# Silu behind its own half of the projections, final sums and store in halves, and one chunk's statistics moved behind the scan loop

## What is computed

```python
x = x + 0.5 * moe(layernorm(x))       # silu(x @ Wg.T) * (x @ Wu.T) @ Wd.T, weighted per expert
x = x + scan_block(layernorm(x))
x = x + 0.5 * moe(layernorm(x))
x = x + 0.5 * ffn(layernorm(x))       # (silu(x @ Wg.T) * (x @ Wu.T)) @ Wd.T
x = x + attention(layernorm(x))
x = x + 0.5 * ffn(layernorm(x))
```

## Time and profile before

| | us |
|---|---|
| median of the 3 runs | 1901.24 |
| lowest and highest | 1899.95, 1901.25 |
| the profiled execution, its own time | 1902.52 |
| its span, first to last instruction | 1900.7 |
| PE busy | 1808.4 (95%) |
| DVE busy | 1333.8 (70%) |
| ACT busy | 945.2 (50%) |
| POOL busy | 581.2 (31%) |

### The profile page before, as it was taken

How to read it: one execution, slowest core, us unless ns; L and a number is a source line. 1 busy time by engine, 2 the same in 40 slices (tenths; PEclk the granted TensorE clock), 3 DMA queues, 4 the chain that set the end, 5 groups by cost and what they waited for, 6 DMA issues and landing times.

```text
span 1900.7 us, 26241 instructions
## 1 busy us (share of the span) xinstructions
PE 1808.4 (95%) x9417; PEld 1375.2 (72%) x9417; DVE 1333.8 (70%) x1870; ACT 945.2 (50%) x1782; POOL 581.2 (31%) x399
## 2 busy tenths in 40 slices
PE   7999999999799999988689999999999999999998
PEld 6888888888354544534267888888888887777887
DVE  6666656567999999999976666565675556666533
ACT  3442323333688677684445433233333338888422
POOL 1000234000489878888720000000000025555000
PEclk9999999999899999999999999999999999999999
DMA  5332344220222222223202233232121306553100
GB/s 197 90 98 66 97 145 136 64 62 23 67 73 70 69 72 77 71 71 108 72 17 76 72 95 105 65 104 63 64 77 44 65 1 147 109 109 68 37 12 23
DMA packets 84186, 146.39 MB, mean 77 GB/s; under 512 B 13848, under 2 KB 23704, under 8 KB 83544
## 3 DMA queue, kind: packets, MB, share of 16 engines
q1 hardware_dynamic: 84056, 144.72, 26.6%
HBM read 130.38 MB, written 14.29 MB: 76 GB/s over the span
## 4 chain that ended last, share of the span: by engine, by line
PE 72%; DVE 14%; issue 6%; ACT 4%; POOL 3%; DMA 0%; DVEq 0%; SPq 0%; POOLq 0%; ACTq 0%
PE psum L161 19%; PE psum L162 18%; PE psum L163 18%; DVE scan_state L1618 6%; PE psum L1437 5%; POOL scan_state L1208 2%; PE psum L1990 1%; PE psum L1361 1%; DVE scan_state L1625 1%; PE psum L1332 1%; ACT attn_p L2138 1%; DVE X L807 1%; DVE moe_hidden_lo L850 1%; PE psum L1421 1%; PE psum L278 1%
## 5 line engine op out<-in xcount | busy, mean ns | idle before, releaser
L1208 POOL TENSOR_TENSOR scan_state<-scan_delta_u,scan_B_rows 128x1024 f32<-128x1024 f32 x127 | 299.5, 2368 | 95.3 <-PE psum L1437 81.2
L161 PE MATMUL psum<-xnT_hi,moe_w_hi 128*128 128x512 f32 x800 | 316.5, 396 | 2.7 <-DVE xnT_lo L470 2.6
L778 ACT ACTIVATE moe_hidden<-psum 128x512 f32<-128x512 f32 x200 | 119.5, 597 | 393.9 <-PE psum L163 393.9
L162 PE MATMUL psum<-xnT_lo,moe_w_hi 128*128 128x512 f32 x800 | 314.2, 393 | 0.0
L163 PE MATMUL psum<-xnT_hi,moe_w_lo 128*128 128x512 f32 x800 | 312.0, 390 | 0.0
L1618 DVE TENSOR_TENSOR_SCAN scan_state<-psum,scan_state 128x1024 f32<-128x1024 f32 x128 | 292.2, 2283 | 4.2 <-POOL scan_state L1208 3.0
L827 DVE TENSOR_TENSOR moe_gated_up<-moe_gate_rows,psum 128x512 f32<-128x512 f32 x184 | 126.5, 688 | 210.0 <-PE psum L163 124.8
L1437 PE MATMUL psum<-scan_state,ident 128*128 128x512 f32 x512 | 248.1, 608 | 3.8 <-DVE scan_gated L1633 2.6
L418 POOL TENSOR_SCALAR rstd<-mean_var 128x2 f32<-128x2 f32 x48 | 10.5, 220 | 752.8 <-DVE mean_var L452 752.5
L161 PE MATMUL psum<-moe_w_hi,moe_hidden_hi 128*128 128x256 f32 x800 | 230.4, 288 | 3.9 <-DVE moe_hidden_lo L850 2.6
L163 PE MATMUL psum<-moe_w_hi,moe_hidden_lo 128*128 128x256 f32 x800 | 226.3, 283 | 0.0
(11 more groups left out here) (226 smaller groups left out, 3476.4 us busy)
## 6 DMA issues: line engine op xcount, KB each, us to landing
scan_B_rows<-scan_B SPq DMA_DIRECT2D x127, 256.0 KB, 3.1
moe_gate_rows<-gate_table SPq DMA_DIRECT2D x176, 128.0 KB, 3.0
moe_w_raw<-moe_pack SPq DMA_DIRECT2D x50, 384.0 KB, 4.0
attn_stack<-attn_rows SPq DMA_DIRECT2D x96, 128.0 KB, 5.3
moe_gate_rows<-gate_table SPq DMA_DIRECT2D x32, 224.0 KB, 3.1
ffn_w_raw<-ffn_pack SPq DMA_DIRECT2D x16, 384.0 KB, 3.6
moe_gate_rows<-gate_table SPq DMA_DIRECT2D x32, 160.0 KB, 2.6
moe_gate_rows<-gate_table SPq DMA_DIRECT2D x24, 192.0 KB, 2.8
```

Of the source, the lines that this page charges most:

```text
L161: e.matmul(out, wH, xH, start=start, stop=False)
L162: e.matmul(out, wH, xL, start=False, stop=False)
L778: e.activation(self.hb[:, b, :], self.k.psum[:, 2 * b, :], ACT.Silu).then_inc(self.s_silu.sem, 1)
L1208: e.tensor_tensor(self.st[q % self.NBUF][:], self.dtu[:, 2 * h:2 * h + 2, :], self.Bs[:, q % self.RING, :].unsqueeze(1).broadcast_to([P, 2 ...
```

## The change

It has three parts. (1) In every Glu step the gate half of the projection raises a semaphore of its own, `s_gs`, and Silu waits for that; the multiplication of line 835 now waits for `s_gu` too. (2) In the last stage the last `down` raises `s_half` after its sixth matmul, and the last `take` adds half 0 behind that and half 1 behind `s_dn`; the last chunk is stored by two transfers of 256 KB, each behind its own add. (3) The statistics of chunk 1 of the tail between scan and second MoE leave the scan loop: DVE does them after the last `gate`, before the last adds; POOL's part goes to the start of the MoE stage's list, and ACT's normalisation (line 293, four instructions) behind the Silu of the MoE stage's step 0.

```diff
--- before.py
+++ after.py
@@ -404,11 +404,16 @@
 
     def sync(self, e):
 
-        for c in range(NCH):
+        for c in range(NCH - 1):
             e.wait_ge(self.s_add.sem, self.s_add.at(2, c))
             e.dma_start(self.out[c * CHUNK:(c + 1) * CHUNK, :].rearrange("(n p) f -> p n f", p=P),
                         self.k.X[:, 4 * c:4 * c + 4, :]).then_inc(self.s_store.sem, 16)
-        e.wait_ge(self.s_store.sem, 16 * NCH)
+        for p in range(2):
+            e.wait_ge(self.s_add.sem, self.s_add.at(p + 1, NCH - 1))
+            rows = slice((TILES - 4 + 2 * p) * P, (TILES - 2 + 2 * p) * P)
+            e.dma_start(self.out[rows, :].rearrange("(n p) f -> p n f", p=P),
+                        self.k.X[:, TILES - 4 + 2 * p:TILES - 2 + 2 * p, :]).then_inc(self.s_store.sem, 16)
+        e.wait_ge(self.s_store.sem, 16 * (NCH + 1))
 
     def pool(self, e, c, slot):
         if slot in (0, 2) and not self.last:
@@ -531,12 +536,14 @@
         self.s_wH = Sem(k, "wH", total=self.tiles)
         self.s_wL = Sem(k, "wL", total=self.tiles)
         self.s_gu = Sem(k, "gu", total=N)
+        self.s_gs = Sem(k, "gs", total=N)
         self.s_silu = Sem(k, "silu", total=N)
         self.s_tu = Sem(k, "tu", total=len(self.gated)) if gates else None
         self.s_h = Sem(k, "h", total=N)
         self.s_hH = Sem(k, "hH", total=N)
         self.s_hL = Sem(k, "hL", total=N)
         self.s_dn = Sem(k, "dn", total=N)
+        self.s_half = Sem(k, "dn_half") if tail.last else None
         self.s_acc = Sem(k, "acc", total=NCH * (self.NG - 1))
         a = Arena(k, tag)
         if gates:
@@ -654,7 +661,7 @@
             self.tail.sync(e)
 
     def pool(self, e):
-        for c in range(2 if self.guest else NCH - 1 if self.handed else NCH, NCH):
+        for c in range(1 if self.guest else NCH - 1 if self.handed else NCH, NCH):
             for slot in (0, 2):
                 self.before.pool(e, c, slot)
         for c in range(NCH - 1 if self.hands or self.lends else NCH):
@@ -678,7 +685,7 @@
                 w = slice((half * KB + kb) * P, (half * KB + kb + 1) * P)
                 m = three(e, k.psum[:, b + half, :], self.wH[slot][:, w], self.wL[slot][:, w],
                           k.xH[:, kb, cols], k.xL[:, kb, cols], kb == 0, kb == KB - 1)
-        m.then_inc(self.s_gu.sem, 1)
+            m.then_inc((self.s_gu if half else self.s_gs).sem, 1)
 
     def down(self, e, j):
         g, c, t = self.place(j)
@@ -691,6 +698,8 @@
             m = three(e, self.sums(n // 2)[:, (n % 2) * HID:(n % 2 + 1) * HID], self.hH[:, j % 2, rows],
                       self.hL[:, j % 2, rows], self.wH[slot][:, w], self.wL[slot][:, w], t == 0 and n % 2 == 0,
                       end and n % 2 == 1)
+            if n == 1 and self.tail.last and j == self.N - 1:
+                m.then_inc(self.s_half.sem, 1)
         m.then_inc(self.s_dn.sem, 1)
 
     def sums(self, p):
@@ -772,7 +781,7 @@
         for j in range(self.N):
             b = j % 2
             self.splits(self.split_hi, e, j)
-            e.wait_ge(self.s_gu.sem, self.s_gu.at(j + 1))
+            e.wait_ge(self.s_gs.sem, self.s_gs.at(j + 1))
             if j >= 2:
                 e.wait_ge(self.s_hL.sem, self.s_hL.at(j - 1))
             e.activation(self.hb[:, b, :], self.k.psum[:, 2 * b, :], ACT.Silu).then_inc(self.s_silu.sem, 1)
@@ -799,10 +808,16 @@
     def take(self, e, n):
 
         c, last = n % NCH, n - NCH * (self.NG - 1)
-        e.wait_ge(self.s_dn.sem, self.s_dn.at(self.ends(n)))
+        by_half = self.tail.last and n == NCH * self.NG - 1
+        if not by_half:
+            e.wait_ge(self.s_dn.sem, self.s_dn.at(self.ends(n)))
         if n >= NCH:
             self.taken(e, n - NCH)
         for p in range(2):
+            if by_half and p == 0:
+                e.wait_ge(self.s_half.sem, self.s_half.at(1))
+            elif by_half:
+                e.wait_ge(self.s_dn.sem, self.s_dn.at(self.N))
             x = self.k.X[:, 4 * c + 2 * p:4 * c + 2 * p + 2, :].rearrange("p j f -> p (j f)")
             m = e.scalar_tensor_tensor(x, self.sums(p), 0.5, x, ALU.mult, ALU.add)
             if last >= 0:
@@ -831,6 +846,7 @@
                 e.tensor_tensor(self.hb[:, b, :], self.hb[:, b, :], self.tu[:, b, :],
                                 ALU.mult).then_inc(self.s_h.sem, 1)
             else:
+                e.wait_ge(self.s_gu.sem, self.s_gu.at(j + 1))
                 e.wait_ge(self.s_silu.sem, self.s_silu.at(j + 1))
                 e.tensor_tensor(self.hb[:, b, :], self.hb[:, b, :], k.psum[:, 2 * b + 1, :],
                                 ALU.mult).then_inc(self.s_h.sem, 1)
@@ -1002,6 +1018,12 @@
         if self.LOGITS.get(j) == 0:
             e.wait_ge(t.s_add.sem, t.s_add.at(2, NCH - 1))
         super().pe(e, j)
+
+    def act(self, e, j):
+        if j == 0:
+            for p in range(2):
+                self.tail.act(e, 1, 2 * p)
+        super().act(e, j)
 
 
 class Scan:
@@ -1231,8 +1253,8 @@
                 e.wait_ge(self.s_bc.sem, self.s_bc.at(c + 2))
             if self.next and q in (self.N - 5, self.N - 4):
                 self.next.split_lo(e, q + 5 - self.N)
-            if c == NCH - 1 and r in (7, 14, 22, 24):
-                self.tail.pool(e, r // 20, 2 * (r in (14, 24)))
+            if c == NCH - 1 and r in (7, 14):
+                self.tail.pool(e, 0, 2 * (r == 14))
         if not self.next:
             for slot in (0, 2):
                 self.tail.pool(e, NCH - 1, slot)
@@ -1587,8 +1609,8 @@
                 log(c, 1)
             if r == 23 and c + 1 < NCH:
                 log(c + 1, 0)
-            if c == NCH - 1 and r in (9, 16, 24, 26):
-                self.tail.act(e, r // 20, 2 * (r in (16, 26)))
+            if c == NCH - 1 and r in (9, 16):
+                self.tail.act(e, 0, 2 * (r == 16))
             if r == 27 and c + 1 < NCH:
                 rows_hi(c + 1)
             if q == self.N - 8 and self.next:
@@ -1677,9 +1699,11 @@
             weigh(q)
             if q and r % NST == 0:
                 gate((q - 1) // self.UNITS, 0 if r else 1)
-            if c == NCH - 1 and r in (5, 12, 21, 23):
-                self.tail.stats(e, r // 20, int(r in (12, 23)))
+            if c == NCH - 1 and r in (5, 12):
+                self.tail.stats(e, 0, int(r == 12))
         gate(NCH - 1, 1)
+        for p in range(2):
+            self.tail.stats(e, 1, p)
         for p in range(2):
             add(NCH - 1, p, self.ENDS[p])
         if not self.next:
```

## The result

The changed kernel takes 1896.5 us (median of 8 runs, 1895.62 to 1899.26), the kernel before 1901.6 us beside it (8 runs, 1899.95 to 1905.45). The ratio is 0.9972, 95% interval 0.9962 to 0.9981: about 5 us faster. The forecast was 1896.3 us, with 1895.0 to 1898.4 as its range.

A forecast was written before the change was run, and what follows sets the result against it. DVE was taken to bound the scan loop, PE the MoE and FFN, with nothing overlapping at the very end. Statistics -2.0, Silu -1.7, adds -0.64 and store -0.6 sum to -4.9 us: 1901.24 to 1896.3 us, range 1895.0 to 1898.4.

The forecast's parts named there:

- What would show it: Trace signs listed beforehand for right (units of 3.46 us, shorter waits, landing about 2.2 us) and for wrong.
- more than worked out: First FFN's 1.71 us wait falls away whole and MoE openings give some tenths: 1894.9 us; chance 0.06.
- Statistics, -2.0: Scan loop: each half's statistics cost DVE 1.00 us, both leave the loop, no cost at the new place; -2.0 us.
- The rival: Second MoE's opening: PE waits for late x_stage of chunk 1, all 2.0 us returned, 1898.3 us; chance 0.08.
- Silu, -1.7: FFN stages: earlier Silu starts the multiplication 0.57 us sooner, counted at three long PE waits; -1.7 us.
- Adds, -0.64: Kernel's end: half 0's add runs beside the second six matmuls, leaving one add behind the last; -0.64 us.
- Store, -0.6: Last store: 256 KB lands in 2.2 us where 512 KB took 2.8; -0.6 us.
- the rival: Last store: second half waits behind the first and lands after 2.8 us, no gain, 1896.9 us; chance 0.10.
- The slower rival, signal inside the projection: Signal after the sixth matmul of 264 steps costs PE time; at 0.04 us each 10.6 us, 1906.9; chance 0.04.

The follow-up runs named there:

- the fourteen profiles: Profiles of the kernel before, the changed kernel and the follow-up kernels, all cut at the same five rows; by stretch the change sums to -6.2 us.
- the two later comparisons: The changed kernel run again, nothing edited, against the kernel before: ratios 0.9958 and 0.9966.
- Silu alone: Kernel before with only the earlier signal, so Silu waits for its half of the projection; against the kernel before: ratio 0.998, -3.8 us.
- statistics alone: Kernel before with only the second half-chunk's statistics, POOL's chain and ACT's normalisation moved behind the last gate; against the kernel before: ratio 0.9986, -2.7 us.
- the wait alone: Kernel before with only the extra wait for gu ahead of L835, no second signal; against the kernel before: ratio 1.0009, +1.7 us.

## Why the prediction was right, and where it was not

**What it forecast and what came.** 1896.3 against 1896.5, and each sign of "What would show it" is there: units of 3.46, a wait of 2.93 for the first add, L278 without a gap, L851 released by PE, the three waits, an add beside the last down product. Against the fourteen profiles the forecast of -4.9 us is too small by about 1.3, and by the ratios of the two later comparisons the time would have been 1893 to 1895, below the low end of the range. So the rival *more than worked out*, at 0.06, got too little: with 1894.9 it lies nearer than the forecast. That 1896.3 met 1896.5 within 0.2 us is luck: the base, 1901.24 as the median of three, was low (1901.6 in the first comparison, 1903.0 to 1903.8 in the later ones), and the gain was put too small.

**Statistics, -2.0**: right, -2.0 in the scan (2.02 between the profiles of Silu alone and statistics alone, neither of which has a slow stretch that costs a unit time). The third MoE's opening takes nothing back: ACT's normalisation ended at 974.85, forecast 976.5, and PE needed it at 977.43. The rival falls.

**Silu, -1.7**: the mechanism was right, the size wasn't: -2.8. Two terms stood at zero. The first is the step ahead of the first FFN's wait, where before's timeline of PE has a hole too small for my threshold of 0.1 us:

```profile
1423.89 0.40 PE L163 MATMUL psum<-xnT_hi,ffn_w_lo 128*128 128x512 f32 x1
1424.37 0.39 PE L161 MATMUL psum<-ffn_w_hi,ffn_hidden_hi 128*128 128x256 f32 x1
```

With Silu alone the same two stand 0.24 apart instead of 0.48:

```profile
1419.98 0.40 PE L163 MATMUL psum<-xnT_hi,ffn_w_lo 128*128 128x512 f32 x1
1420.22 0.28 PE L161 MATMUL psum<-ffn_w_hi,ffn_hidden_hi 128*128 128x256 f32 x1
```

and with the shorter first matmul that is 0.34 us. The second is "In the shared first tiles the MoE openings wait for other chains; I take 0": the first MoE's opening gained 0.5, of which the wait ahead of L278 at 20.77 (0.24, gone) is one piece and the wait ahead of L334 at 108.27 (0.21, then 0.12) another; the rest I didn't trace. At the third MoE's opening a like gain (the wait of 0.25 at 985 is gone) pays for the 0.26 that DVE's extra wait costs behind it. The three long waits shrank by 0.62 to 0.63 instead of 0.57: L835 starts on PE's signal as soon after it as Silu did, not 0.06 later as line 827 does.

**Adds, -0.64**: -0.63, which is the tail's -1.35 less the store's 0.72. **Store, -0.6**: -0.72. Its landing is 2.1 us, forecast 2.2. Both halves land 2.1 us after their issue, where 512 KB take 2.8, so the second doesn't pay for the first, and the rival falls. The rule of the Trainium skill (DMA: Bandwidth & Descriptors, Rules for kernel authors), that two transfers to disjoint partition halves serialise, isn't about this case, though the prediction set it against the split: the two stores split the tokens, and each takes all 128 partitions. Nor is the fit of the Trainium skill that the prediction used (same page, Anatomy of one DMA) for these transfers: the page gives it for those that POOL issues, and by it the estimates were 3.2 and 2.6 us for stores by SP that took 2.8 and 2.1.

**The slower rival, signal inside the projection**: its mechanism falls, as the rows show no x. The FFN stage of 32 steps takes 138.18 and 138.19 us with the signal and 138.19 with the wait alone. What the prediction had not priced is the wait instruction that comes with it on DVE: 0.06 us a time where DVE is on the path, and the 0.34 at 1052. In the changed kernel the first is not seen, the second is there (0.46 at 1049.18, 0.21 at 1051.51 before).

**What stays open**: why kernels with the added signal and wait, but the late Silu, measure 1.7 to 3.0 us slower when 0.6 can be found in rows; whether the change also makes the slow stretches that cost time rarer (the scan's means are 468.4 with the statistics in it and 465.3 without, 3.1 apart where 2.0 are the change's; the rest is ten stretches of 1.68 against six, 0.96, and 0.19 in the third unit, and seven profiles of each kind can't tell ten from six); and why L385 is late.

## What to carry to other kernels

Price a wait at the last link of its chain, and go through the small holes of the bounding engine as well: those under 0.35 us held about 0.8 of the 1.3 us that were missing here. A single profile of each kernel can differ by more than the change does; cut all profiles at the same rows and compare stretch by stretch, since stretches that no draw touches (tail, FFN stage) resolve 0.05 us where medians resolve 2. And look on what a slow instruction runs beside before it is split: moving POOL's additions off DVE's norm brought another 1.1 us, and that version beats the kernel before by its ratios and the changed one by its rows.

## What the runs showed of the hardware

- TensorE's granted clock falls to half at a few places of this kernel. Where the scan opens and PE waits 9.28 us it does so in all fourteen profiles, for 10 to 14 us. Elsewhere it falls for some 3 us where PE has just had short waits (0.61 of 2 us busy at 614 to 616), mostly in only some of the executions. Such a stretch near 616, 736 or 852 cost 1.68 us in a stage that DVE bounds, and one near 876 or 936 nothing. In the attention stage one near 1570 alone goes with 0.2 to 0.5 us (196.64, 196.89 and 196.75 against 196.41 without any), the later ones with 1.4 to 2.6.
- At the start PEclk reads 1.00 in the windows from 12 to 18 us, while the matmuls stand 0.43 instead of 0.23 us apart, for a time that varies by execution. The column doesn't show this phase: the trace's first clock record starts at 15.5 to 18.8 us, when it is over, and where there is no record the column reads 1.00. The Trainium skill (TensorE: Matmul & The Clock Gate, The HAM clock gate) says that the number of slow matmuls at the start varies from run to run of one kernel, and the fourteen profiles agree (six to twelve).
- DVE's normalisation of two row blocks takes 0.73 us alone and 4.41 beside POOL's addition of two tensors. The Trainium skill (SBUF — State Buffer, SBUF: two separate sides) has the port pair that the two engines share as a lock, held for a whole instruction; the trace agrees, as each of DVE's two instructions ends 0.15 us behind one of POOL's, and with POOL elsewhere the 3.7 us are gone.
- One instruction more in DVE's list made another, unrelated one 0.36 us late at one place, in every kernel that had it.
